# One layer of a graph network: weighted sums over edges from dense matrices on TensorE in place of row gathers

## The reference

```python
h = max(layernorm(x), 0)
x += L0(h): per source: sum, max, mean of edge_attr_32; two dense layers
x += L1(h): sums of h[src] per target; a dense layer
x += L2(h): (1 + eps) * h + segment_sum(where(src != dst, edge_weight, 0)[:, None] * h[dst], src)
x += L3(h): twice: a = segment_sum(W [hv[dst], hv[src], edge_attr_64] + b, dst); a gated cell
```

## Time and profile before

| what | value |
|---|---|
| runs | 6448.43 us median of 3 (6443.69 to 6449.52) |
| span of the profiled execution | 6441.6 us |
| PE / DVE / ACT / POOL busy | 57% / 64% / 19% / 56% |
| mean granted TensorE clock | 0.685 of full |
| DMA | 634.91 MB, 99 GB/s over the span |

### The profile page before, as it was taken

The page is one execution under the profiler, slowest core; times in us unless marked ns, Lnnn a source line. Parts: engine busy times, 40 slices in busy tenths (PEclk is TensorE's granted clock), DMA queues, the critical chain, the costliest instruction groups (busy, mean ns, idle before and its releaser), DMA issues. The chain is left out here.

```text
span 6441.6 us, 115669 instructions
## 1 busy us (share of the span) xinstructions
PE 3666.2 (57%) x27862; PEld 2870.0 (45%) x27863; DVE 4108.0 (64%) x11121; ACT 1238.9 (19%) x3929; POOL 3600.3 (56%) x3398
## 2 busy tenths in 40 slices
PE   4377778778778778740017686554432222210988
PEld 3234555555555555530017686554432222210977
DVE  8888877777777777769630577775554444432333
ACT  0023444444444444420010000000000000000111
POOL 0025777777777777740230277777777777763000
PEclk5588887887888887865559655555555555555999
DMA  1001211211111211127509344443333233321977
GB/s 25 2 20 35 63 53 51 63 53 52 61 54 52 63 53 52 61 78 286 182 17 426 108 99 100 102 95 78 87 76 71 58 69 69 69 50 62 386 292 269
DMA packets 459644, 634.91 MB, mean 99 GB/s; under 512 B 342019, under 2 KB 397479, under 8 KB 426087
## 3 DMA queue, kind: packets, MB, share of 16 engines
q1 hardware_dynamic: 347202, 493.86, 23.4%
q0 software_dynamic: 106624, 86.11, 6.5%
q10 hardware_dynamic: 5670, 53.26, 2.2%
HBM read 420.15 MB, written 212.81 MB: 98 GB/s over the span
## 5 line engine op out<-in xcount | busy, mean ns | idle before, releaser
L414 POOL DMA_INDIRECT sorted_rows<-rows,place_i x1568 | 1813.7, 1157 | 801.3 <-issue 462.6
L1349 POOL DMA_INDIRECT gathered_rows<-feature_table,gather_index x1568 | 1579.3, 1007 | 501.5 <-issue 463.0
L1435 PE MATMUL block_total<-attr_half,block_hot 128*128 128x65 f32 x4048 | 876.2, 418 | 320.0 <-DMA attr_half<-in_edge_attr_dram 304.5
L1435 PEld LDWEIGHTS block_total<-attr_half,block_hot 128*128 128x128 f32 x4048 | 867.2, 332 | 329.0 <-issue 309.9
L595 PE MATMUL part<-high,low 128*128 x3520 | 916.8, 392 | 118.3 <-DVE high L466 109.7
L466 DVE TENSOR_TENSOR high<-iota_g,window_keys 128x1568 f16 x880 | 850.8, 967 | 0.3
L580 PE MATMUL count_rows<-counts,lo_rows_f 128*128 128x49 f32 x3136 | 718.5, 320 | 0.0
L1393 DVE TENSOR_SCALAR block_hot<-iota_f,block_keys 128x128 f32<-128x128 f32 x2024 | 502.7, 302 | 183.5 <-PE block_total L1435 61.4
L595 PEld LDWEIGHTS part<-high,low 128*128 x3520 | 379.6, 108 | 484.9 <-issue 347.9
L580 PEld LDWEIGHTS count_rows<-counts,lo_rows_f 128*128 128x128 f32 x3136 | 579.5, 230 | 25.2 <-issue 21.0
L1404 DVE TENSOR_TENSOR_SCAN gathered_rows<-same_src,sum_carry,gathered_rows 128x32 f32<-128x32 f32 x3136 | 578.2, 266 | 6.3
(11 more groups left out here) (352 smaller groups left out, 5510.7 us busy)
## 6 DMA issues: line engine op xcount, KB each, us to landing
piece_round<-slabs SPq DMA_DIRECT2D x98, 1568.0 KB, 9.1
slabs<-slab SPq DMA_DIRECT2D x49, 1568.0 KB
piece_conv<-slabs SPq DMA_DIRECT2D x49, 1568.0 KB, 23.0
attr_half<-in_edge_attr_dram SPq DMA_DIRECT2D x184, 352.0 KB
scanned<-scan_out ACTq DMA_DIRECT2D x8, 6272.0 KB, 29.7
scanned<-gathered_rows SPq DMA_DIRECT2D x49, 1024.0 KB, 5.1
scan_rows<-sorted_rows SPq DMA_DIRECT2D x8, 3430.0 KB, 29.6
sorted_rows<-rows,place_i POOLq DMA_INDIRECT x1568
```

The source lines that it names most:

```text
L414: pool.indirect_dma_start(sorted_rows[:, :], bass.IndirectOffsetOnAxis(ap=place_i[:, h, u:u + 1], axis=0), rows[:, h, u, :], None).then_in ...
L1349: pool.indirect_dma_start(got[b][:, j, :], None, table[:, :], bass.IndirectOffsetOnAxis(ap=index[b][:, j:j + 1], axis=0)).then_inc(gathere ...
L1435: nc.tensor.matmul(total[b][:, :], hot[:, j, :], attr[j // HALF][:, j % HALF, :], start=False, stop=True, skip_group_check=True).then_inc( ...
```

## The change

**Message stage.** `feature_table`, `scan_messages` and `blk_table` go. Sources are cut into 44 chunks of 144 (`CSRC`), each of 48 windows of 3 sources. A pass (`weighted_sums`) takes up to 128 edges of each window of a chunk; a chunk with a fuller window takes two passes. The passes are laid out at run time, their number made even. One pass does the following.

- POOL fetches 48 runs of 128 records (key, low part of the target, weight) with one gathering DMA, two passes ahead (`fetch`), and multiplies four tiles of 1536 elements (`third_w`, L1628), adds one 128 x 144 result into `weighted_agg` (`add`).
- PE turns the records (three transposes), builds the dense matrix [6272 targets x 144 sources] as 4 batches of 12 windows x 3 parts = 36 products of 147 columns (16-bit; the 32-bit weight is split in three parts), and applies it one pass later: 49 products of `weighted_h` (64 columns) with 144 columns of 32-bit values, in two pieces of 24 and 25 set between batches.
- DVE makes for each batch the one-hots `equal` (1536) and `high` (1764) and the first weight part (1536), and for batch 0 the second one as well (1536), all 16-bit; `take_keys` prepares 8 small operands (128 x 48).
- ACT makes the second weight part for batches 1 to 3 (36 products of 128 x 128) and copies the 16 banks of 441 columns out of PSUM.
- The sums of `edge_attr_64` per target come from scans in target order: 32 steps, one in each of passes 2 to 33, of 64 scans over 50 elements on 125 partitions, 32 behind batch 1 and 32 before batch 3. SP loads and stores them.

**Elsewhere.** `prepare_keys` makes the record's fields (16 long operations in, three out); `ROW` is 36; `find_ranges` loses the blocks' part; `scan_sorted` loses L686 to L688, and ACT copies and stores the records there; `edge_statistics_layer` lays out the passes (`pass_index`, `pass_base`) on SP, PE and DVE, behind one iota on POOL ahead of the gathers; `find_dst_runs` and a second `locate_runs` run before the passes; `gather_runs` then fetches attribute sums, while PE turns `weighted_agg` and DVE adds it to x; `sum_unsorted` runs only for unsorted targets.

```diff
@@ prepare_keys, DVE
-            nc.vector.tensor_copy(g["sdw"][:, :, 2], raw_w[:, :]).then_inc(dve_step, 1)
+            nc.vector.tensor_copy(src_f[:, :], raw_i[:, 0, :]).then_inc(dve_step, 1)
+            nc.vector.tensor_single_scalar(part_i[:, :], raw_i[:, 1, :], 7, ALU.arith_shift_right).then_inc(dve_step, 1)
+            nc.vector.tensor_single_scalar(lo_i[:, :], raw_i[:, 1, :], P - 1, ALU.bitwise_and).then_inc(dve_step, 1)
+            step(nc.vector.tensor_tensor(w_p, src_p, key_p, ALU.not_equal))
+            step(nc.vector.tensor_tensor(w_p, w_p, raw_w[:, :], ALU.mult))
+            step(nc.vector.tensor_copy(lo_p, lo_i[:, :]))
...
@@ scan_sorted, ACT
+                nc.scalar.copy(record[k % 2][:, :, :], rows[k % 2][:, :, DA + 1:ROW]).then_inc(record_made, 1)
+                act.wait_ge(record_made, k + 1)
+                act.dma_start(records_v[:, k * J:(k + 1) * J, :], record[k % 2][:, :, :]
+                              ).then_inc(records_out[k % 2], 16)
@@ edge_statistics_layer, POOL
-            gather_runs(nc, pool, g, scanned, carries, ends, carry_in, gathered)
+            pool.iota(pass_i[:, :], pattern=[[1, QM]], base=0, channel_multiplier=0).then_inc(pass_iota, 1)
+            gather_runs(nc, pool, g["end_i"], g["end_part_i"], scanned, carries, ends, carry_in, gathered)
@@ weighted_sums, POOL (in place of scan_messages)
+            def body(q, b, scan, since):
+                pool.wait_ge(turned_ready, q + 1)
+                fetch(q + 2, b)
+                for j in range(NBATCH):
+                    pool.wait_ge(equal_ready, q * NBATCH + j + 1)
+                    pool.tensor_tensor(low[2][j % 2][:, :, :, :], equal[j % 2][:, :, :, :], pair_keys(third_w[b], j, P),
+                                       ALU.mult).then_inc(third_made, 1)
+                    if j == 2 and since:
+                        add(q - 1, 1 - b)
@@ weighted_sums, DVE
+            def batch(q, b, j):
+                k = j % 2
+                dve.wait_ge(bank_ready, q * BANKS + 4 * j - 4 + AHEAD)
+                if j == 0:
+                    dve.wait_ge(keys_ready, q + 1)
+                nc.vector.tensor_tensor(equal[k][:, :, :, :], iota(P), pair_keys(row[b], j, P), ALU.is_equal
+                                        ).then_inc(equal_ready, 1)
+                nc.vector.tensor_tensor(high[k][:, :, :, :], iota(KEYS), pair_keys(column[b], j, KEYS), ALU.is_equal)
+                dve.wait_ge(equal_ready, q * NBATCH + j + 1)
+                if j == 0:
+                    nc.vector.tensor_tensor(low[1][k][:, :, :, :], equal[k][:, :, :, :], pair_keys(second_w[b], j, P),
+                                            ALU.mult)
+                nc.vector.tensor_tensor(low[0][k][:, :, :, :], equal[k][:, :, :, :], pair_keys(first_w[b], j, P),
+                                        ALU.mult).then_inc(made, 1)
...
+            def body(q, b, scan, since):
+                batch(q, b, 0)
+                batch(q, b, 1)
+                if scan is not None:
+                    scans(scan, b, 0, D // 2)
+                batch(q, b, 2)
+                take_keys(q + 1, 1 - b)
+                if scan is not None:
+                    scans(scan, b, D // 2, D)
+                batch(q, b, 3)
+                if scan is not None:
+                    keep_carry(scan, b)
@@ weighted_sums, PE
+            def build(q, j):
+                k = j % 2
+                pe.wait_ge(made, q * NBATCH + j + 1)
+                if j:
+                    pe.wait_ge(second_made, q * (NBATCH - 1) + j)
+                pe.wait_ge(third_made, q * NBATCH + j + 1)
+                for n in range(4):
+                    pe.wait_ge(bank_copied, q * BANKS + 4 * j + n + 1)
+                    for w in range(3):
+                        pair, side = divmod(3 * n + w, 2)
+                        for part in range(3):
+                            last = nc.tensor.matmul(bank[n][:, w * KEYS:(w + 1) * KEYS], low[part][k][:, pair, :, side],
+                                                    high[k][:, pair, :, side], start=part == 0, stop=part == 2,
+                                                    skip_group_check=True)
+                    last.then_inc(bank_ready, 1)
...
+                for a in range(first, last):
+                    side = a % 2 * D
+                    end = nc.tensor.matmul(ps_agg[b][side:side + D, 0:CSRC], h[:, a, :], dense[b][:, a, :], start=False,
+                                           stop=True, skip_group_check=True)
...
+            def body(q, b, scan, since):
+                build(q, 0)
+                build(q, 1)
+                turn(q + 1, 1 - b)
+                if since:
+                    apply(q - 1, 1 - b, 0, 24)
+                build(q, 2)
+                if since:
+                    apply(q - 1, 1 - b, 24, NB)
+                build(q, 3)
```

More of the change, by code:

```diff
@@ L51 @@
 KEY_SCALE = 1.0 / 8
+WS = 3
+CW = 48
+CSRC = CW * WS
+NCH = -(-N // CSRC)
+KEYS = WS * NB
+GB = 12
+NBATCH = CW // GB
+BANKS = CW // 3
+QPART = 404
+QM = 4 * QPART
+NO_PASS = float(1 << 22)
+PASS_COL = 64
+EP2 = 125
+RPP = E // EP2
+J2 = 50
+STEPS2 = RPP // J2
 RANGES = "the ranges are worked out within the tiles"
@@ L616, in _, with scan_sorted @@
                             window(i, (h * RG + u) // 2, before)
[L619 removed]
+def scan_sorted(nc, g, sorted_rows, scanned, carries, records):
     J = 196
@@ L631, in scan_sorted @@
         cap = s.sb("cap", [EP, J], F32)
-        differs = s.sb("differs", [EP, J], F32)
+        same_src = s.sb("same_src", [EP, J], F32)
+        record = [s.sb(f"record{b}", [EP, J, 3], F32) for b in range(2)]
         last_key = s.sb("last_key", [EP, 1], F32)
@@ L649, in scan_sorted @@
         shifted = s.sem("shifted")
+        record_made = s.sem("record_made")
+        records_out = [s.sem(f"records_out{b}") for b in range(2)]
         carried = s.sem("carried")
@@ L670, in _ @@
             act.wait_ge(rows_out[1], 16 * (STEPS // 2))
+            for b in range(2):
+                act.wait_ge(records_out[b], 16 * (STEPS // 2))
         @block.vector
@@ L724, in _, with locate_runs @@
             nc.tensor.transpose(ps_in[:, :], state[:, :], g["ident"][0:2 * DA, 0:2 * DA]).then_inc(pe_done, 1)
-def locate_runs(nc, g):
-    with Scope(nc) as s:
+def locate_runs(nc, turn, start, deg, per, end_i, part_i, has, spans):
+    with Scope(nc, turn) as s:
         end = s.sb("end", [P, HI], F32)
@@ L1325, in scan_messages, with passes @@
         carried = s.sem("carried")
-        consts = s.sem("block_consts")
-        attr_in = [s.sem(f"attr_in{b}") for b in range(2)]
-        rest_in = s.sem("rest_in")
-        rest_made = s.sem("rest_made")
+        block = s.block()
+        attr_v = edge_attr_64.rearrange("(p j) c -> p (j c)", p=EP2)
+        out_v = scanned[0:E, :].rearrange("(p j) c -> p (j c)", p=EP2)
+        def passes(engine, name, body, between=None):
+            body(0, 0, None, 0)
+            body(1, 1, None, 1)
+            with engine.Fori(0, SCANS) as i:
+                for b in range(2):
+                    body(2 * i + 2 + b, b, 2 * i + b, 2)
+            if between is not None:
+                between()
+            count = one_value(nc, g["pass_count"][0:1, 0:1], name, LEAST, MOST)
+            with engine.Fori(SCANS, count) as i:
+                for b in range(2):
+                    body(2 * i + 2 + b, b, None, 2)
+            return 2 * count + 1
@@ new lines, in _ @@
+        @block.tensor
+        def _(pe):
+            pe.sem_inc(used, 1)
+            pe.sem_inc(copied, 1)
+            with rounds(pe, PE):
+                with pe.Fori(0, NB) as b:
+                    pe.wait_ge(copied, b + 1)
+                    nc.tensor.matmul(total[:, :], g["zerob"][:, 0:P], g["zerob"][:, 0:D], start=True, stop=True)
+                    with pe.Fori(0, STEPS2) as k:
+                        pe.wait_ge(attr_in, (b * STEPS2 + k) * 16 + 16)
+                        pe.wait_ge(made, b * STEPS2 + k + 1)
+                        for j in range(J2):
+                            last = nc.tensor.matmul(total[:, :], hot[:, j, :], attr[:, j, :], start=False, stop=True,
+                                                    skip_group_check=True)
+                        last.then_inc(used, 1)
@@ L1469, in weighted_layer @@
-def weighted_layer(nc, g, table, scanned, carries, eps, edge_attr_64):
+            with rounds(act, ACTE):
+                with act.Fori(0, NB) as b:
+                    act.wait_ge(used, b * STEPS2 + STEPS2 + 1)
+                    nc.scalar.copy(g["attr_sum"][:, bass.ds(b * (D + 1), D)], total[:, :]).then_inc(copied, 1)
+def weighted_layer(nc, ctx, g, records, scanned, carries, dst, eps, edge_attr_64):
+    agg = ctx.enter_context(nc.sbuf_tensor("weighted_agg", [P, NCH * CSRC], F32))
+    g["attr_sum"] = agg[:, 0:NB * (D + 1)]
@@ L1499, in _ @@
             def _(pool):
-                gather_runs(nc, pool, g, scanned, carries, ends, carry_in, gathered)
```

(13 more changed lines are left out.)

732 lines of the change are left out of this document (503 added, 229 removed).

## The result

| | before | changed |
|---|---|---|
| median, same chip | 6446.06 us of 4 runs (6440.76 to 6449.52) | 62399.63 us of 4 runs (62397.79 to 62411.2) |
| ratio | | 9.684, 95% interval 9.670 to 9.698 |
| span of the profiled execution | 6441.6 us | 62397.8 us |

The account below looks back on a forecast made before the run. POOL's 1568 gathers were taken to bound the message stage. Replacing its 2122.4 us gave 6448.4 - 2122.4 + 44 (around the passes) + 4 (elsewhere) + 1535 (passes) = 5909 us, range 5580 to 6420.

Parts of the forecast that it names:

- sum_unsorted reads one flag on each engine and meets: Final part: the fallback for unsorted targets costs only a flag read and a meeting of engines, +2.5 us (1 to 5).
- rival 3: Message stage: PE at 1.2 GHz with 32-bit weight loads not hidden, 51 us a pass, kernel 6720 us; chance 0.12.
- VectorE's work, 27.7 us a pass: Message stage: VectorE's products, small operations, scans and carry take 27.7 us in a pass with scans, 13.4 without.
- POOL's product, 2.1 us: Message stage: a POOL product of 1536 elements takes 2.1 us, the middle between 1.4 and 2.8.
- VectorE and POOL exclude each other: Message stage: the two engines' work adds up, 27.7 + 8.9 = 36.6 us with scans, 13.4 + 8.9 = 22.3 without.
- rival 1: Message stage: POOL does not hold up VectorE, passes of 29 and 24 us, kernel 5638 us; chance 0.30.
- its own sign of being wrong: Message stage: the prediction is wrong if VectorE waits for bank_ready more than a few us a pass.
- The pass, 36.6 and 26 us: Message stage: 32 passes with scans at 36.6 us and 14 at 26, PE limiting the latter, 1535 us together.
- rivals 2 and 3: Message stage: PE stays at 1.2 GHz; with loads hidden kernel 6370 us, chance 0.13; with them not hidden 6720, chance 0.12.
- ScalarE, 14.6 to 18 us: Message stage: ScalarE's 36 products and 16 copies take 14.6 us a pass, or 18, hidden behind VectorE and PE.
- The entry, 22 + 8 us: Ahead of the passes: find_dst_runs and locate_runs with meetings take 22 us, the first pass's preparation before batch 0 takes 8.
- Elsewhere, +4: Outside the message stage: gains and losses in prepare_keys, find_ranges, scan_sorted, edge_statistics_layer, the final block and sum_unsorted sum to +4 us.

Follow-up runs that it names:

- flag_zero: Changed kernel with the flag that sum_unsorted reads written as constant 0, loops kept: 62752.62 us in one run.
- bounded_blocks: Changed kernel with the end of sum_unsorted's loop over 49 blocks set to 49 times the flag: 7232.16 us in one run.
- no_fallback: Changed kernel with the call of sum_unsorted left out: 6072.19 us, ratio 0.9421 to the kernel before.
- third_on_dve: As no_fallback, with the product of the weight's third part made by VectorE instead of POOL: 5708.37 us, ratio 0.8855 to the kernel before.
- add_last: As no_fallback, with POOL's addition of the last pass's sums put behind its product of batch 3: 5988.84 us, ratio 0.9299 to the kernel before.
- guarded_by_counts: As third_on_dve, with the fallback kept and its first turn made small and harmless: 5721.24 us, ratio 0.8891 to the kernel before.
- copies_first: As third_on_dve, with ScalarE copying a batch's banks before the next second part in passes with scans: 5698.81 us, ratio 0.8841 to the kernel before.

## Why the prediction was wrong, point by point

**The step that failed is one sentence**: "sum_unsorted reads one flag on each engine and meets: +2.5 (1 to 5)". It took the loop over 0 or 1 turns for a condition. It is not one: the body runs before the count is looked at, and in place of 2.5 us it cost 56325.6. flag_zero and bounded_blocks show this, and no_fallback shows that nothing else is in the excess. No rival held it; rival 3, the slower one, was priced at 6720. The place to look was the program, not the trace: where a loop's comparison stands, and line 858 of the kernel before. The body's price was never worked out; at 1568 steps of a 6400-element comparison and 100 matmul records even a small chance for it was worth a rival.

**The rest of the sum, against no_fallback: 6072 where 5909 was forecast.** By the mark, the weighted layer lost 390.7 us (2282.6 to 1891.9) where the steps give 2122.4 - 44 - 1535 + 3.4 = 546.8.

- *46 passes*: right. POOL's product has 184 records, four a pass.
- *VectorE's work, 27.7 us a pass*: right. In third_on_dve, with four products of 0.87 more, it is busy 30.9 of 32 us. Its operations took 0.87 and 0.99 as worked out; 2048 scans average 304 ns as recorded and stand 0.22 apart (32 in 7.04 us).
- *POOL's product, 2.1 us*: mis-sized. 2.75 alone, 3.30 on average. The upper bound of 2.8, in which the second input costs as much as the first, was the right choice. The Trainium skill's figure (GPSIMD Engine Reference, Performance versus the Vector engine), measured there on an addition of 2048 32-bit elements and as an estimate 3.4 us at 1536, is 0.6 above the undisturbed product here. The passes of 42 and 27.7 us (27.5 by the prediction's own terms) and the 6106 us worked out from it lie close to the measured 40.2, 27.4 and 6072. That is luck: they count each product as time that VectorE is held, which is not how the time was spent.
- *VectorE and POOL exclude each other*: right as a mechanism, and rival 1 falls. VectorE's one-input conversion of 48 elements (L1700) took 2.33 us beside a product and 0.18 otherwise, its product 3.50 against 0.95. The Trainium skill (SBUF — State Buffer, Who interferes with whom) states this of VectorE operations with two SBUF inputs, and the rows agree; it says that `tensor_scalar` can hold the shared ports as well when it runs in a two-port mode, which fits L1700, whose mode no row shows. The sum of the two engines' work was the wrong form, though: two of POOL's four products ran while VectorE waited anyway (4429.02 and the one behind it), so exclusion cost VectorE 2.55 + 2.15 us in a pass with scans, and the rest of the pass was a chain.
- *The chain that was missed*: POOL's addition of the last pass stood ahead of the product of batch 3 and waited 14.5 us for ScalarE's copy of the sums; PE waited 9.2 us for that product, and VectorE 8.5 for PE. The prediction asked of ScalarE's store in `scan_sorted` what it could hold up, and did not ask it of `add(q - 1)`; its own sign of being wrong, VectorE waiting more than a few us a pass for `bank_ready`, came true with these 8.5. Taking the addition out of the way was worth 83 us (add_last), and taking POOL's products out of the chain 280 more (third_on_dve).
- *The pass, 36.6 and 26 us*: 40.2 and 27.4, so 32 x 3.6 + 14 x 1.4 = 135 of the missing 156 us. The 26 came near by luck. It was worked out with PE as the limit of a pass without scans; PE was busy 20.1 of 27 us there (no_fallback, columns as in the earlier trace rows), and the pass fell to 24.3 and 21.1 us when POOL's wait and then its products went (add_last, third_on_dve).

```profile
5090.00:5117.00 27.00, 20.11 (x246) 18.96 (x246) 18.45 (x21) 19.13 (x53) 13.57 (x8) 0.87 0.01 3
```

- *PE*: it never was the bound. Granted clock 0.76 with scans and 0.86 without (no_fallback, 5030 to 5330), so between its two levels, and rivals 2 and 3 (1.2 GHz throughout) fall. In the fastest rows 36 16-bit products took 2.63 us, 73 ns each where 66 was taken. The 32-bit products were mis-sized the other way: 98 records, one whole application, took 6.34 us (timeline of no_fallback), 65 ns each where 120 was taken. A pass's work at full clock is then 4 x 2.63 + 6.3 + 0.8 = 17.6 us and not 21.8. Why these records are cheaper for their width than those of the earlier trace rows is not shown.

```profile
5370.14 6.34 PE L1800 MATMUL ps_agg<-dense,weighted_h 128*64 128x144 f32 x98
```

- *ScalarE, 14.6 to 18 us*: 12 products in 3.65 and 4 copies in 1.97 make 18.8.
- *The entry, 22 + 8 us*: 43.8 (3649.3 to the first one-hots at 3693.1), of which the wait for the targets is 15.6 us where 7 was taken.
- *Elsewhere, +4*: outside the mark no_fallback's span is 18 us longer, of which 16 lie ahead of it. `prepare_keys` was sized too low: the first one-hots of `count_sources` come 25 us later than before (74.1 against 49.1) where 19 was taken, and the first scatter of `rank_and_build` 16.7 later (397.6 against 380.9) where 9 was. The scatters then last between 2456.5 us (guarded_by_counts) and 2471.9 (copies_first) in kernels whose code there is the same, so the rest is not settled.

Without the fallback the time, 6072 us, lies inside the stated range, but the pass that gives it is made up otherwise than the forecast's.

## What to carry to other kernels

Before a condition is priced at nothing, find the instruction that skips the body, and price the body once in full: here the loop tested at its end, and a count of 0 meant one turn. Where a loop must serve as a condition, make its first turn small and harmless (15.6 us here), or keep it out. And where VectorE and POOL share a pass, look at each queue for what stands behind a wait, and weigh four short products more on VectorE (0.87 us each) against the same on POOL (2.75 each, and up to 8.1 when VectorE goes first).

## What the runs showed of the hardware that was not expected

The exclusion is not one wait for one instruction. In batch 3 of add_last POOL's product waited out several VectorE instructions that followed each other, 5.3 us in all, while in batch 1 (4402.11, 3.52 us) it got its turn at the end of the one instruction that ran, and the next of VectorE took 3.50. Which of the two happens is decided by something these runs don't show. Of VectorE's small operations beside a product, those reading the records from PSUM kept their 0.2 to 0.3 us; the one that converts from SBUF was held.

The mean granted clock of a stretch rose together with PE's busy time: 0.76 and 0.75 at 143 and 140 of 260 us busy (no_fallback), 0.82 at 174 and 179 (third_on_dve). The runs show the two rising together and not which drives the other.
